# Attention scores in 64 by 64 products: queries and keys in place of the combined query-key weights

## The chip, the cores and the metric

The kernel runs on one core of one Trainium2 chip. The metric is device time in microseconds (us) for one execution. The time before is the median of three runs. One more execution was profiled, and all rows below come from it.

## What is computed

An audio tower: 64 sequences of 64 steps pass through a signature layer (running sums of outer products up to depth 4), then attention with 8 heads of 64 within each sequence, then a routed feed-forward layer with 8 experts and a shared one. The part that the change touches, cut from the reference:

```python
# h: (64, 63, 128) out of the signature layer; x is its layer norm
qkv = x @ Wq.T                      # Wq = w_qkv / spectral norm * sigma, (1536, 128)
q, k, v = split(qkv, 3)             # each (b, n, 8 heads * 64)
dots = einsum('bhid,bhjd->bhij', q, k) * exp(temperature)
dots = where(eye, NEG_MAX, dots)    # a step does not attend to itself
attn = softmax(dots, axis=-1)
out  = einsum('bhij,bhjd->bhid', attn, v)
h    = h + out @ Wo.T + b_out
```

Per head the score is x Wq' Wk x', which can be had either from queries and keys (64 wide) or from the product Wq' Wk (128 by 128), taken once.

## The kernel before

The 4096 padded steps are 32 tiles of 128 rows; a tile holds two sequences of 64. The kernel is written engine by engine, each with its own order of instructions, and semaphores between them. After a start-up, one loop runs over the tiles, and each `iteration(i, ...)` works on several tiles at once: attention of tile i, projection of the signature features of tile i+2, the level sums and features of tile i+3, and layer norm, router and output of tiles i-1 and i-2. A shared feed-forward stage, then 39 sorted expert slabs, follow. Work sits where the code puts it; no scheduler moves it.

PSUM is eight banks, B[0] to B[7]. The names that matter:

- `weight_products` (L1237) multiplies query and key weights of each head in the start-up, 64 rows of weights at a time into banks 6 and 7; ScalarE copies them to `qkw` (L663). The same helper does the products of value and output weights, which stay.
- In `iteration` of TensorE (L1368): eight products of `qkw` with the tile `xT` into banks 5 and 6 (L1375), which ScalarE scales into `xqk` (L608). The router's logits of tile i-2 go to bank 4 (L1381), and VectorE copies them out (`keep_logits`, L936).
- `three(...)` makes the values-times-output product in halves of 512 columns, three matmuls each: the first into bank 7, the second into bank 5 (L1385, L1387). ScalarE copies both to `xvo` (L613), and SP moves them by head to `xvp` by DMA.
- `project(i + 2, lo, hi)` (L1280) is the projection of the features, cut into ten chunks of two or three matmuls that stand between the attention's steps. `accumulate` (L1316) sums the channels, after GpSimd's tree of additions.
- The scores (L1396): a bf16 matmul writes the mask into bank 4, then for each of the two sequences one fp32 product adds the scores of all eight heads: the 64 columns of `xT` as the loaded operand, 512 columns of `xqk` as the moving one, into 64 rows of the bank.
- VectorE takes the row maximum and subtracts it (L999, L1001), ScalarE the exponential, VectorE the sum and the division. PE transposes the result (L1425) and multiplies it with `xvp` one iteration later (`values`, L1358).
- At tiles 25 to 27 VectorE also does steps of the routing (`choose`, `running`, `place`) at the end of its iteration, and at `RANK_AT` (tile 26) PE ranks the early tiles into bank 6. From tile 28 GpSimd also issues the scatters of the early tiles' rows.

All matmuls go through the helper `mm`, so they share the line L1217.

## Time and profile before

| | us |
|---|---|
| median of three runs | 694.17 |
| the three runs | 692.53, 694.17, 695.29 |
| the profiled execution | 691.94 |
| its span on the core | 690.1 |

In the page PE stands for TensorE's matmuls, PEld for its weight loads, which run beside them. A matmul's end in the records is modelled: its last record's duration holds a tail that the next one overlaps, so the pace of a run of matmuls is read from the starts. In a timeline several like instructions are merged, with "x16" for their number, from the first start to the last end. An fp32 matmul leaves two records of each kind. The bf16 matmul of the mask has a load record, but no matmul record. The clock of TensorE was granted in full in the loop.

### The profile page before, as it was taken

What the parts mean: (1) busy time and instruction counts of PE and PEld (TensorE: products, weight loads), DVE (VectorE), ACT (ScalarE), POOL (GpSimd) and SP (SyncE); (2) the same over time, 40 slices, a digit from 0 to 9 for tenths busy, and PEclk for the clock granted to TensorE, in tenths of its full rate; (3) what the DMA queues carried; (4) which work ended last, traced back from release to release, by engine and by line L of the source; (5) the groups of instructions that cost most, each with busy time, mean ns of one, the idle gap of its engine ahead of it and who ended that gap; (6) DMA issues with size and microseconds to landing.
All of it is one profiled execution on the core that took longest, in us unless ns stands there. A gap on an engine that the chain in (4) does not pass through costs nothing.

```text
span 690.1 us, 13988 instructions
## 1 busy us (share of the span) xinstructions
PE 647.0 (94%) x3964; PEld 519.6 (75%) x3997; DVE 420.6 (61%) x1110; ACT 295.9 (43%) x702; POOL 322.1 (47%) x336
## 2 busy tenths in 40 slices
PE   5999999999999999999999999999789989999993
PEld 4677887788878888788877887776578957777772
DVE  7876666666666666766656666766436235455451
ACT  4234455434544445444454344443646334434340
POOL 2455454544545445444545444448534014545453
PEclk9999999999999999999999999999999999999997
DMA  8611344333634334343343431112354113232230
GB/s 308 270 35 31 78 104 95 90 93 76 146 83 99 84 80 118 77 107 76 93 105 83 100 77 39 34 36 73 99 195 138 43 46 44 37 44 39 39 40 5
DMA packets 70133, 59.70 MB, mean 87 GB/s; under 512 B 6752, under 2 KB 58848, under 8 KB 69728
## 3 DMA queue, kind: packets, MB, share of 16 engines
q1 hardware_dynamic: 63472, 55.21, 30.2%
q0 software_dynamic: 6640, 4.22, 4.4%
q8 instruction: 12, 0.20, 0.1%
q14 instruction: 9, 0.07, 0.0%
HBM read 16.78 MB, written 26.30 MB: 62 GB/s over the span
## 4 chain that ended last, share of the span: by engine, by line
PE 83%; DVE 6%; issue 4%; POOL 4%; DMA 1%; ACT 0%; SPq 0%; ACTq 0%; DVEq 0%; POOLq 0%
PE bank L1217 74%; PE bank L1539 3%; PE bank L1273 2%; PE bank L1426 2%; POOL sorted_rows L485 1%; POOL z L470 1%; PE bank L1522 1%; PE bank L1332 1%; PE bank L1323 0%; PE bank L1278 0%; POOL z L472 0%; PE bank L1277 0%; POOL out L558 0%; DVE utl L777 0%; DVE z L883 0%
## 5 line engine op out<-in xcount | busy, mean ns | idle before, releaser
L1217 PE MATMUL bank<-whigh,uth 128*128 128x512 f32 x512 | 169.1, 411 | 1.2 <-DVE lowt L777 1.2
L1217 PEld LDWEIGHTS bank<-whigh,uth 128*128 128x128 f32 x512 | 92.4, 190 | 28.0 <-issue 7.4
L558 POOL DMA_INDIRECT out<-prob,ids x39 | 60.9, 1561 | 94.0 <-ACT prob L740 92.5
L1217 PE MATMUL bank<-whigh,utl 128*128 128x512 f32 x256 | 101.6, 397 | 0.0
L479 POOL TENSOR_TENSOR rstd<-rstd,powers 128x1 f32<-128x1 f32 x64 | 35.3, 552 | 119.8 <-DVE rstd L870 64.5
L470 POOL TENSOR_TENSOR z<-z 128x512 f32<-128x512 f32 x32 | 42.3, 1323 | 90.9 <-DVE z L883 90.9
L1217 PE MATMUL bank<-xT,qkw 128*128 128x128 f32 x512 | 63.9, 279 | 0.0
L1190 DVE COPY xvp<-bank 128x512 f32<-128x512 f32 x39 | 27.0, 692 | 59.3 <-PE bank L1539 59.3
L1217 PEld LDWEIGHTS bank<-xT,qkw 128*128 128x128 f32 x512 | 61.3, 196 | 0.1
L1217 PEld LDWEIGHTS bank<-whigh,utl 128*128 128x128 f32 x256 | 48.4, 189 | 11.9
L883 DVE TENSOR_TENSOR z<-bank,v 128x512 f32<-128x512 f32 x64 | 44.1, 690 | 20.8 <-PE bank L1217 16.8
L1217 PE MATMUL bank<-whigh,vow 128*128 x117 | 49.0, 526 | 0.0
L628 ACT ACTIVATE prob<-prob 128x512 f32<-128x512 f32 x32 | 20.2, 633 | 66.4 <-DVE prob L1001 63.5
L610 ACT ACTIVATE xqk<-bank,fac 128x512 f32<-128x512 f32 x64 | 43.9, 690 | 7.2 <-PE bank L1217 5.7
L638 ACT COPY pt<-bank 128x512 f32<-128x512 f32 x32 | 18.8, 587 | 64.6 <-PE bank L1426 62.5
L729 ACT ACTIVATE z<-bank 128x512 f32<-128x512 f32 x39 | 23.3, 597 | 49.0 <-PE bank L1217 27.7
L465 POOL TENSOR_TENSOR e3l<-e,e3h 128x512 fp32r<-128x512 f32 x31 | 40.8, 1316 | 7.4 <-DVE xn L904 6.5
L1217 PEld LDWEIGHTS bank<-xvp,pt 128*64 128x64 f32 x512 | 30.1, 137 | 18.3 <-issue 18.3
L1217 PE MATMUL bank<-vow,xTh 128*128 128x512 f32 x128 | 42.9, 416 | 0.0
L892 DVE TENSOR_TENSOR h<-bank,tokb 128x128 f32<-128x128 f32 x32 | 9.3, 290 | 54.4 <-PE bank L1217 54.4
L1217 PE MATMUL bank<-xqk,xT 128*64 128x512 f32 x128 | 34.5, 618 | 8.4 <-DVE logits L938 4.2
L617 ACT COPY xvo<-bank 128x512 f32<-128x512 f32 x64 | 37.6, 587 | 10.5 <-PE bank L1217 8.9
(227 smaller groups left out, 1439.2 us busy)
## 6 DMA issues: line engine op xcount, KB each, us to landing
sorted_rows<-blank SPq DMA_DIRECT2D x24, 709.5 KB, 5.7
xvp<-xvo SPq DMA_DIRECT2D x128, 128.0 KB
w<-w_t SPq DMA_DIRECT2D x1, 4096.0 KB, 12.3
xvo<-sorted_rows SPq DMA_DIRECT2D x39, 64.5 KB, 1.7
w<-w_high SPq DMA_DIRECT2D x4, 512.0 KB, 6.5
x_columns<-x2t SPq DMA_DIRECT2D x32, 64.0 KB
xg_in<-x_columns SPq DMA_DIRECT2D x8, 256.0 KB
levels<-w_t SPq DMA_DIRECT2D x1, 2048.0 KB, 7.5
```

The source lines that it names most:

```text
L465: G.tensor_tensor(e3l[:], e3[:], e3h[:].bitcast(F32), ALU.subtract).then_inc(e3_lo, 1)
L470: G.tensor_tensor(z4[:], z[:, 0:4, :], z[:, 4:8, :], ALU.add).then_inc(tree, 1)
L479: G.tensor_tensor(rstd[:, n, 1:2], rstd[:, n, 0:1], powers[:, 0:1], ALU.pow) \
L558: nc.gpsimd.indirect_dma_start(out=out[:, :], out_offset=bass.IndirectOffsetOnAxis(ap=ids[:, j:j + 1], axis=0), in_=y[:, j % 2, :], in_off ...
L610: A.activation(xqk[:, :, 4 * n:4 * n + 4, :], B[5 + n][:].rearrange("p (s h k) -> p s h k", s=2, h=4), ACT.Copy, scale=fac[:, 1:2]).then_i ...
L617: A.copy(xvo[:, n, :, :].rearrange("p c d -> p (c d)"), B[7 - 2 * n][:]) \
L628: A.activation(prob[:], prob[:], ACT.Exp).then_inc(exp_done, 1)
L729: nc.scalar.activation(act[:, k, :], B[1 + 2 * k][:], ACT.Silu).then_inc(silu_done, 1)
L883: V.tensor_tensor(z[:, cs, :], B[1 + half][:].rearrange("p (c d) -> p c d", c=4), spread(v[:, bass.ds(s, 1), cs].rearrange("p o c -> p (o ...
L1190: V.tensor_copy(hidT[:, k, :, :].rearrange("p c t -> p (c t)"), B[5][:]).then_inc(hT_sb, 1)
L1217: return T.matmul(out_, lhsT, rhs, start=start, stop=stop)
L1539: last = T.transpose(B[5][:, col(c)], hid[:, k, col(c)], ident)
```

## The change

The query-key products of the weights go. Instead the weights for queries and keys are loaded as they are, transposed, into `wqk` (one DMA of 512 KB in SP's queue, ahead of the shared expert's), and each iteration makes queries (bank 5) and keys (bank 6) with eight products of 128 by 128 by 128. ScalarE scales the queries and copies the keys into `qk`, in which a pair of heads takes the two halves of the partitions.

The scores become one fp32 product per head and sequence: 64 by 64 by 64, 16 of them. The head's half of the partitions picks the rows of the array, the sequence its columns, and the heads of a pair write two banks, 5 and 6. The mask is written in two halves into these. VectorE reads the scores from both banks in one instruction; for that the eight banks are one tensor.

Bank 4 is free of scores and takes the second half of the values-and-output product. It also holds the logits, so the wait for their copy (`lg_sb`) moves from the mask to this product, and `project(i + 2, 0, 1)` moves ahead of it. The early ranks go to bank 4.

TensorE, start of a loop iteration, before (`vow` is the values-and-output weight, `whigh` the projection's, `z,sq` the sum over channels, `gateT` the router's):

```order
L1217 MATMUL bank<-xT,qkw 128x2x64 x7
L1335 REGISTER_ALU
L1217 MATMUL bank<-gateT,x2t 128x8 [waits x2T_sb]
L1382 REGISTER_ALU
L1217 MATMUL bank<-vow,xTh 128x512 [waits h2_done,xT_lo]
L1217 MATMUL bank<-vow,xTh 128x512
L1217 MATMUL bank<-vow,xTl 128x512
L1386 REGISTER_ALU
L1217 MATMUL bank<-vow,xTh 128x512 [waits xqk_sb]
L1217 MATMUL bank<-vow,xTh 128x512
L1217 MATMUL bank<-vow,xTl 128x512
```

And after, the same place:

```order
L1218 MATMUL banks<-vow,xTl 128x512
L1281 ISA
L1282 REGISTER_ALU [waits z_sb]
L1283 ISA [waits u4_hi]
L1218 MATMUL banks<-whigh,uth 128x512 [waits u4_lo]
L1218 MATMUL banks<-whigh,uth 128x512
L1218 MATMUL banks<-whigh,utl 128x512
L1218 MATMUL banks<-vow,xTh 128x512 [waits logits_sb]
L1218 MATMUL banks<-vow,xTh 128x512
L1218 MATMUL banks<-vow,xTl 128x512
```

The second `vow` product stood straight behind the first; now the projection's chunk stands between them, and the wait for the logits in front of the second.

TensorE around the scores, before:

```order
L1217 MATMUL bank<-z,sq 128x128 [waits tree]
L1396 MATMUL bank<-mask,ident_b 128x512 [waits logits_sb,xqk_sb]
L1217 MATMUL bank<-xqk,xT 64x512 x2
L1360 ISA [waits xvo_sb]
L1217 MATMUL bank<-xvp,pt 64x128 [waits probT_sb,xvo_by_head]
L1217 MATMUL bank<-xvp,pt 64x128 x7
```

And after:

```order
L1218 MATMUL banks<-z,sq 128x128 [waits tree]
L1394 MATMUL banks<-mask,ident_b 128x256 [waits queries_keys_sb]
L1394 MATMUL banks<-mask,ident_b 128x256
L1218 MATMUL banks<-qk 64x64 x16
L1402 REGISTER_ALU
L1358 ISA [waits xvo_sb]
L1218 MATMUL banks<-xvp,pt 64x128 [waits probT_sb,xvo_by_head]
```

Two wide products have become sixteen narrow ones, and the mask no longer waits for the logits.

The core of the diff:

```diff
@@ SP, loads
+            sp.dma_start(wqk[:].rearrange("p a c m -> p (a c m)"), wqk_t).then_inc(ld_qk, 16)
             sp.dma_start(sw1_in, sw1_t).then_inc(ld_sw, 16)
...
-            sp.wait_ge(ww_psum, 4)
+            sp.wait_ge(ww_psum, 2)
@@ ScalarE, iteration
-                for n in range(2):
-                    a.wait_ge(g_psum, 2 * i + (n + 1))
-                    A.activation(xqk[:, :, 4 * n:4 * n + 4, :],
-                                 B[5 + n][:].rearrange("p (s h k) -> p s h k", s=2, h=4),
-                                 ACT.Copy, scale=fac[:, 1:2]).then_inc(g_sb, 1)
+                a.wait_ge(g_psum, 2 * i + 1)
+                A.activation(qk[:, 0, :, :].rearrange("p c t -> p (c t)"), B[5][:], ACT.Copy,
+                             scale=fac[:, 1:2]).then_inc(g_sb, 1)
+                a.wait_ge(g_psum, 2 * i + 2)
+                A.copy(qk[:, 1, :, :].rearrange("p c t -> p (c t)"), B[6][:]).then_inc(g_sb, 1)
...
-                    A.copy(xvo[:, n, :, :].rearrange("p c d -> p (c d)"), B[7 - 2 * n][:]) \
+                    A.copy(xvo[:, n, :, :].rearrange("p c d -> p (c d)"), B[7 - 3 * n][:]) \
@@ ScalarE, start-up
-            for n in range(2):
-                a.wait_ge(ww_psum, n + 1)
-                A.copy(qkw[:, 4 * n:4 * n + 4, :].rearrange("p h d -> p (h d)"), B[6 + n][:]).then_inc(qkw_sb, 1)
@@ VectorE, iteration
-                sc = B[4][:].rearrange("p (c k) -> p c k", k=LEN)
-                V.tensor_reduce(rowmax[:], sc, AX, ALU.max).then_inc(soft, 1)
+                sc = banks[:, 5:7, 0:PAIRS * LEN].rearrange("p n (c k) -> p n c k", k=LEN)
+                row_max = rowmax[:].rearrange("p (n c) -> p n c", n=2)
+                V.tensor_reduce(row_max, sc, AX, ALU.max).then_inc(soft, 1)
                 d.wait_ge(soft, i + 1)
-                V.tensor_tensor(prob[:], sc, spread(rowmax[:], 2, [P, HEADS, LEN]), ALU.subtract) \
+                V.tensor_tensor(prob[:].rearrange("p (c n) k -> p n c k", n=2), sc,
+                                spread(row_max, 3, [P, 2, PAIRS, LEN]), ALU.subtract) \
                     .then_inc(shifted, 1)
@@ TensorE, iteration
-                for hd in range(HEADS):
-                    by_head = B[5 + hd // 4][:].rearrange("p (s h k) -> p h s k", s=2, h=4)
-                    last = mm(by_head[:, hd % 4, :, :], qkw[:, place(hd), :], xT[:])
-                    if hd % 4 == 3:
-                        last.then_inc(g_psum, 1)
+                for n in range(2):
+                    for c in range(PAIRS):
+                        last = mm(B[5 + n][:, col(c)], wqk[:, n, c, :], xT[:])
+                    last.then_inc(g_psum, 1)
...
                 three(B[7][:], x, [vow[:, n, 0:512] for n in range(2)]).then_inc(vo_psum, 1)
-                pe.wait_ge(g_sb, 2 * i + 1)
-                three(B[5][:], x, [vow[:, n, 512:] for n in range(2)]).then_inc(vo_psum, 1)
                 if u:
                     project(i + 2, 0, 1)
+                if prev and older:
+                    pe.wait_ge(lg_sb, i - 1)
+                three(B[4][:], x, [vow[:, n, 512:] for n in range(2)]).then_inc(vo_psum, 1)
                 if acc:
                     accumulate(i + 1)
                 pe.wait_ge(g_sb, 2 * i + 2)
-                if prev and older:
-                    pe.wait_ge(lg_sb, i - 1)
-
-                T.matmul(B[4][:], ident_b[:], mask[:], start=True, stop=False)
-                for s in range(2):
-                    last = mm(B[4][col(s, LEN), :], xT[:, col(s, LEN)],
-                              xqk[:, s, :, :].rearrange("p h k -> p (h k)"), False, True)
+
+                for n in range(2):
+                    half_ = slice(n * PAIRS * LEN, (n + 1) * PAIRS * LEN)
+                    T.matmul(B[5 + n][:, 0:PAIRS * LEN], ident_b[:], mask[:, half_], start=True, stop=False)
+                for c in range(PAIRS):
+                    for n in range(2):
+                        head = col(n, HEAD_DIM)
+                        for s in range(2):
+                            last = mm(B[5 + n][col(s, LEN), col(c, LEN)], qk[head, 0, c, col(s, LEN)],
+                                      qk[head, 1, c, col(s, LEN)], False, c == PAIRS - 1)
                 last.then_inc(s_psum, 1)
...
-                    mm(B[6][:, 0:n], below, oh_early[:].rearrange("p t e -> p (t e)"))
-                    mm(B[6][:, n:2 * n], ones, oh_early[:].rearrange("p t e -> p (t e)")).then_inc(rank_psum, 1)
+                    pe.wait_ge(vo_sb, 2 * i + 2)
+                    mm(B[4][:, 0:n], below, oh_early[:].rearrange("p t e -> p (t e)"))
+                    mm(B[4][:, n:2 * n], ones, oh_early[:].rearrange("p t e -> p (t e)")).then_inc(rank_psum, 1)
@@ TensorE, start-up
-            weight_products(B[6:8], PAIRS, wqkv_sb[:, 0:PAIRS, :])
...
-            pe.wait_ge(qkw_sb, 2)
...
+            pe.wait_ge(ld_qk, 16)
```

## Rows read from the trace of the kernel before

**Rows 1.** The page, the chain that ended last, shares of the span by engine.

```profile
PE 83%; DVE 6%; issue 4%; POOL 4%; DMA 1%; ACT 0%; SPq 0%; ACTq 0%; DVEq 0%; POOLq 0%
```

**Rows 2.** The chain in 200:240: shares by line, then start, duration, what.

```profile
by line: PE bank L1217 91.2%; PE bank L1273 3.0%; PE bank L1426 2.2%; issue 1.1%; PE bank L1323 0.8%; PE bank L1278 0.8%; PE bank L1277 0.8%; PE bank L1332 0.6%
...
204.93 4.73 PE bank L1217 x31
...
219.17 4.73 PE bank L1217 x31
```

**Rows 3.** Timeline of one iteration: start, us, engine, line, what [idle before <- releaser].

```profile
214.53 1.95 PE L1217 MATMUL bank<-xT,qkw 128*128 128x128 f32 x16
...
217.24 0.63 PE L1217 MATMUL bank<-vow,xTh 128*128 128x512 f32 x2
...
217.95 0.63 PE L1217 MATMUL bank<-whigh,uth 128*128 128x512 f32 x2
...
219.17 0.20 PEld L1217 LDWEIGHTS bank<-xqk,xT 128*64 128x64 f32 x4 [0.32 <-issue]
219.17 1.08 PE L1217 MATMUL bank<-xqk,xT 128*64 128x512 f32 x4
...
220.08 1.04 PE L1217 MATMUL bank<-xvp,pt 128*64 128x128 f32 x16
...
221.05 0.30 PEld L1217 LDWEIGHTS bank<-whigh,uth 128*128 128x128 f32 x2 [0.17 <-issue]
...
221.75 0.63 ACT L628 ACTIVATE prob<-prob 128x512 f32<-128x512 f32 x1 [1.94 <-DVE prob L1001]
```

**Rows 4.** Scores' records in 10 ns windows: window, length, busy (x records in it).

```profile
219.19:219.20 0.01, 0.01 (x2) 0.01 (x2) 0.00 (x0) 0.00 (x0) 1.00 0.00 0
...
219.63:219.64 0.01, 0.01 (x2) 0.00 (x0) 0.00 (x0) 0.00 (x0) 1.00 0.00 0
219.67:219.68 0.01, 0.01 (x4) 0.00 (x0) 0.00 (x0) 0.00 (x0) 1.00 0.00 0
```

**Rows 5.** The values' records in such windows: PE, then PEld, DVE, ACT.

```profile
220.18:220.19 0.01, 0.01 (x2) 0.01 (x2) 0.00 (x0) 0.00 (x0) 1.00 0.00 0
220.20:220.21 0.01, 0.01 (x4) 0.01 (x4) 0.00 (x0) 0.00 (x0) 1.00 0.00 0
...
220.31:220.32 0.01, 0.01 (x6) 0.01 (x4) 0.00 (x0) 0.00 (x0) 1.00 0.00 0
```

**Rows 6.** Timeline of the start-up: PE's wait, ScalarE's copies, and products of 64 rows.

```profile
11.59 0.47 PE L1217 MATMUL bank<-e3h,before_r 128*128 128x512 f32 x1 [1.15 <-DVE e3l L847]
...
16.73 1.09 ACT L665 COPY qkw<-bank 128x512 f32<-128x512 f32 x2
...
20.81 1.16 PE L1217 MATMUL bank<-woutT,w 64*128 64x128 f32 x16
...
20.81 0.97 PEld L1217 LDWEIGHTS bank<-woutT,w 64*128 64x128 f32 x16 [0.36 <-issue]
```

**Rows 7.** Values of the last tile in 10 ns windows, right after a DMA wait.

```profile
501.36:501.37 0.01, 0.01 (x3) 0.01 (x4) 0.00 (x0) 0.00 (x0) 1.00 0.00 0
501.39:501.40 0.01, 0.01 (x4) 0.01 (x3) 0.00 (x0) 0.00 (x0) 1.00 0.58 205
```

**Rows 8.** Waits of PE in 400:510: total us, times, longest.

```profile
PE bank L1217 <- DVE logits L938: 4.2, 3, 1.5
```

**Rows 9.** Timeline: VectorE's low features and a logits copy, with PE's next load.

```profile
216.34 0.62 DVE L777 TENSOR_TENSOR lowt<-bank,lowt 64x128 fp32r<-64x128 f32 x2
...
450.89 0.17 DVE L938 COPY logits<-bank 128x8 f32<-128x8 f32 x1
...
451.17 0.10 PEld L1396 LDWEIGHTS bank<-mask,ident_b 128*128 128x128 bf16 x1 [1.32 <-issue]
```

**Rows 10.** The chain in 455:482: where it leaves PE and comes back.

```profile
460.54 0.70 DVE z L883
...
479.08 0.50 PE bank L1217 x2
```

More of the change, by code:

```diff
@@ L89, in build @@
 def build(nc, x_next, x_prev, w_low, w_high, tok_b, wqkv, u_qkv, wout_t, u_columns, b_out,
-          scalars, gate_t, w13_t, w2_t, sw1_t, sw2_t, square, mask_c, steps, out):
+          scalars, gate_t, wqk_t, w13_t, w2_t, sw1_t, sw2_t, square, mask_c, steps, out):
     with ExitStack() as ctx:
@@ L112, in build @@
         tokb = sb("tokb", [P, DIM])
-        qkw = sb("qkw", [P, HEADS, DIM])
+        wqk = sb("wqk", [P, 2, PAIRS, P])
         vow = sb("vow", [P, 2, HEADS * DIM], F32R)
@@ L182, in build @@
         xTl = sb("xTl", [P, P], F32R)
-        xqk = sb("xqk", [P, 2, HEADS, LEN])
+        qk = sb("qk", [P, 2, PAIRS, P])
         xvo = sb("xvo", [P, 2, PAIRS, DIM])
@@ L230, in build @@
                      prob[:].rearrange("p a b -> p (a b)"), z4[:].rearrange("p a b -> p (a b)"))
-        wide = (z[:].rearrange("p c d -> p (c d)"), xqk[:].rearrange("p a b c -> p (a b c)"),
+        wide = (z[:].rearrange("p c d -> p (c d)"), qk[:].rearrange("p a b c -> p (a b c)"),
                 xvp[:].rearrange("p a b c -> p (a b c)"), tail)
@@ L272, in build @@
         y = late(2, DIM)
-        B = [ctx.enter_context(nc.psum_tensor(f"bank{n}", [P, 512], F32)) for n in range(8)]
-        ld_x, ld_before, ld_sq, ld_c, ld_w, ld_wo, ld_sn, ld_w13, ld_w2, ld_sw = (
+        banks = ctx.enter_context(nc.psum_tensor("banks", [P, 8, 512], F32))
+        B = [banks[:, n, :] for n in range(8)]
+        ld_x, ld_before, ld_sq, ld_c, ld_w, ld_wo, ld_sn, ld_qk, ld_w13, ld_w2, ld_sw = (
             sem(f"loaded_{n}") for n in ("x", "before", "square", "const", "attention", "attention_out", "norms",
-                                       "w13", "w2", "shared"))
+                                       "query_key", "w13", "w2", "shared"))
         ld_sig = [sem(f"loaded_signature{c}") for c in range(UC + 1)]
@@ L284, in build @@
         w_hi, w_lo = sem("signature_weights_hi"), sem("signature_weights_lo")
-        ww_psum, ww_hi, ww_lo, qkw_sb = (sem("weight_products_psum"), sem("value_out_weights_hi"),
-                                         sem("value_out_weights_lo"), sem("query_key_weights"))
+        ww_psum, ww_hi, ww_lo = (sem("weight_products_psum"), sem("value_out_weights_hi"),
+                                 sem("value_out_weights_lo"))
         sw_hi, sw_lo = sem("shared_weights_hi"), sem("shared_weights_lo")
@@ L300, in build @@
         xT_hi, xT_lo = sem("xT_hi"), sem("xT_lo")
-        g_psum, g_sb, vo_psum, vo_sb = sem("xqk_psum"), sem("xqk_sb"), sem("xvo_psum"), sem("xvo_sb")
+        g_psum, g_sb, vo_psum, vo_sb = sem("queries_keys_psum"), sem("queries_keys_sb"), sem("xvo_psum"), sem("xvo_sb")
         s_psum, soft, shifted, exp_done = sem("scores_psum"), sem("row_max"), sem("shifted"), sem("exp_done")
@@ L630, in iteration @@
                     a.wait_ge(rank_psum, 1)
-                    A.copy(ranks_early.rearrange("p n m -> p (n m)"), B[6][:, 0:2 * EARLY * EXPERTS]) \
+                    A.copy(ranks_early.rearrange("p n m -> p (n m)"), B[4][:, 0:2 * EARLY * EXPERTS]) \
                         .then_inc(rank_kept, 1)
@@ L668, in _ @@
             for n in range(2):
-                a.wait_ge(ww_psum, n + 3)
+                a.wait_ge(ww_psum, n + 1)
                 A.copy(vow[:, 0, n * 512:(n + 1) * 512], B[5 - n][:]).then_inc(ww_hi, 1)
@@ L1220, in col @@
                 return slice(c * n, (c + 1) * n)
-            def place(hd):
-                return hd % 2 * PAIRS + hd // 2
             pe.wait_ge(ld_before, 16)
@@ L1589 @@
 _IN = ["x_next", "x_prev", "w_low", "w_high", "tok_b", "wqkv", "u_qkv", "wout_t", "u_columns",
-       "b_out", "scalars", "gate_t", "w13_t", "w2_t", "sw1_t", "sw2_t", "square", "mask_c", "steps"]
+       "b_out", "scalars", "gate_t", "wqk_t", "w13_t", "w2_t", "sw1_t", "sw2_t", "square", "mask_c", "steps"]
 def kernel(x, L0_tok_W, L0_tok_b, L0_attn_w_qkv, L0_attn_u_qkv, L0_attn_sigma_qkv, L0_attn_w_out,
@@ L1637 @@
         "gate_t": np.asarray(L0_ffn_gate_w).T,
+        "wqk_t": wqkv[:2 * INNER].T,
         "w13_t": np.concatenate([w1, w3], axis=1).transpose(2, 0, 1),
```

## The prediction

> **What bounds the kernel now.** First the page: TensorE (PE) holds 83% of the chain that ended last [rows 1]. An average hides stages, so next the chain inside the tile loop: PE's lines are nearly all of it, 91.2% the matmul helper's alone, and the same piece comes back after 14.24 us (204.93 to 219.17) [rows 2]. In the loop, then, time is what PE's queue takes, in order; work taken from VectorE or ScalarE gives nothing. The third view is PE's row of one iteration [rows 3], where the edited parts can be priced. Fourth come the places where PE is not the bound: three stalls of 4.2 us in all on the copy of the logits (L938) [rows 8], and a stretch from 460.54 to 479.08 in which the chain leaves PE for VectorE and GpSimd [rows 10].
>
> **What a pass is.** An fp32 matmul shows as two loads and two matmuls, two passes. The eight projections at 214.53 are 16 passes in 1.95 us less the 0.27 of the last one's tail, 0.112 us each for 128 columns [rows 3]. The change keeps eight products of 128x128x128 there, so this part costs what it did. The two output runs of 64 become one of 128; a pair of the values' passes, which write one run of 128, steps 0.11 too [rows 5], so I take nothing.
>
> **The scores before.** Four passes of 512 columns into 64 output rows. At 219.19 two are in progress, at 219.63 still two, at 219.67 four [rows 4]: both halves of the columns of the array stream together, and the second pair starts at about 219.65. The next product's load stands at 220.08, so a pair of passes streams 0.43 us, and the first took 0.05 more because its load was not hidden (219.17 to 219.65). From load to load: 219.17 to 220.08, **0.91 us**.
>
> **The scores after.** 16 products of 64x64x64, 32 passes of 64 columns, on four quarters of the array. The nearest rows are the values' products (two column halves, 128 columns a pass): two in progress at 220.18, four at 220.20, six at 220.31, so a pair starts every 0.11 us [rows 5], and the 16 passes take 1.04 less the last tail of 0.27 [rows 3]. The other split, by rows, stands in the start-up: 16 passes with 64 rows of weights each, into two banks, loads over 0.97 us, matmuls over 1.16 less 0.27, so 0.12 a pair at the most with the first load in it, and loads of 128 columns overlap each other there as well [rows 6]. So each kind of half runs at the pace of its own stream with the other half beside it. What no row shows is both splits at once. Bounds: if all four quarters stream together, a step is half of 0.11, as 64 is half of 128 columns, and 32 passes are 8 steps, 0.44 us. If no quarter overlaps another, a pass costs 0.055 (the same 0.11 over two), 1.76 us. I take the lower end: the rows show both splits free of each other, and the two starts of a pair lie within 0.02 us [rows 5].
>
> Around them the array changes its shape once more than before. After the values' last pair (start 220.08 + 7 x 0.11 = 220.85, end 0.11 later, 220.96) the next load waits until 221.05 [rows 3]: 0.09 for the change, and 0.05 for a load of 64 columns that nothing hides, as at 219.17. So from score load to values' stream: 0.05 + 0.44 + 0.09 + 0.05 = 0.63 against 0.91, 0.28 less. I give back 0.02 for the mask, which is now two matmuls of 256 in place of one of 512 with one more load, and 0.02 for four starts a step in place of two. **Gain 0.24 us an iteration.**
>
> The Trainium skill, "TensorEngine Tiling (Array Packing)", section Key Properties, says that a change of tiling mode drains the engine; the trace agrees, and the 0.09 above is its price here.
>
> **Where it counts.** Iterations 0 to 28 run at PE's pace; 29 begins at about 461, and it and 30 lie in the stretch that GpSimd's scatters set [rows 10]; 31 may count or not. 29 x 0.24 = **7.0 us**.
>
> **What the new order costs.** Before, the three stalled iterations did the second half of the values-and-output product (three passes, 217.24 to 217.95 in the ordinary iteration, 0.71) [rows 3] and the sum of the channels (0.22, two passes of 0.11) ahead of the wait for the logits, beside VectorE's routing steps. Now bank 4 holds that product, so the wait stands in front of it, and both come after the release: 0.93 us each, **3 x 0.93 = 2.8 us** lost. VectorE's release itself does not move: its chain starts from the transposes of the iteration before. In the ordinary iteration the logits' copy stands right behind the remainders that end at 216.96 [rows 9], and takes 0.17, and the wait, now due at 217.95, costs nothing; behind it in PE's queue stand the sum, the masks and the scores.
>
> The first chunk of the projection moves ahead of that product, from 217.95 to 217.24. It needs the last low part of the features, and VectorE ends that at 216.34 + 0.62 = 216.96. PE sees an end of VectorE 0.11 us later (450.89 + 0.17 = 451.06, then 451.17) [rows 9], so the load can start at 217.07 and, at 0.11, is in by 217.18: 0.06 us ahead. I take nothing, but this cover is thin.
>
> ScalarE's second copy to xvo comes some 0.7 us later, and behind it the low features, keep_x2 and the cast of e3. All of these had slack: the exponential that follows them waited 1.94 us for VectorE [rows 3]. SP's second pair of head moves is queued behind a wait for the attention of the tile before, which ends later than that copy. The key copy needs no scale and ScalarE is off the path: nothing. The banks 5 and 6 are now also the scores' banks: PE's next write to them waited for the transposed probabilities already, which come after VectorE's reads. VectorE reads as many elements as before.
>
> **Start-up.** Removed: 16 passes on PE, ahead of a wait of 1.15 us for VectorE at 11.59 [rows 6], so hidden; two ScalarE copies, 1.09 us from 16.73, beside PE and VectorE, which then do other work [rows 6]; and the wait for them. Added: one load of 512 KB in SP's queue, one issue ahead of the shared weights, long before its first use at 44. Bounds: 0 to 1.1 us gained. I take 0.
>
> **Sum.** -7.0 + 2.8 = -4.2 us. The profiled execution took 691.94 us (span 690.1 and 1.84 around it), 2.23 under the median of the three runs; the difference is of the same size for both, so from the median: 694.17 - 4.2 = **690.0 us**.
>
> **Rivals.**
> *Two at a time.* The queue gives a pass only so fast, or lets only two tiles run together. Where PE's queue was empty, after a DMA wait, the partner of a pair came 0.03 us behind: three in progress at 501.36, four at 501.39 [rows 7]. At 0.03 a pass 32 passes are 0.96 us; at half of 0.055, 0.88 us. Against it: where PE came from other work, partners start within 0.02 [rows 5], and in the ordinary iteration no wait ends in the 1 us ahead of the scores. With 0.88, 0.44 more than taken, -0.24 becomes +0.20, 29 x 0.20 = 5.8, plus 2.8: +8.6, 702.8 us; with 0.96, 705.1 us. **This one is slower than before.** It decides from 0.018 us a pass: 32 of them are 0.58, the group 0.81 with the terms above, 0.10 under 0.91, and 29 x 0.10 only pays the 2.8 back.
> The Trainium skill, "TensorE: Matmul & The Clock Gate", section "Wait — 56ns, not 53.3ns?", has a rule that speaks for it: successive matmuls start no closer than about 25 ns however few columns they have. Taken for every pass, that is 0.80 us for the scores, an estimate from that page, and some 700 us in all; its chance is within this rival's. The pairs of [rows 5] start closer than that, so between two halves the trace does not bear it out; for four quarters no row here shows it.
> *One at a time.* 32 x 0.055 = 1.76: 1.32 more than taken, +1.08 an iteration, 31.3 + 2.8, 728 us. For it: products with both splits are in no row. Against: each split alone overlaps fully.
> *A new wait takes the gain.* The 0.06 us ahead of the moved chunk turns negative by 0.05 to 0.15, in 27 iterations 1.4 to 4 us: 691.4 to 694.0, no change. For it: the chain transposes, ScalarE's two casts, VectorE's three remainders has no slack of its own.
> *It does not do what it says*: the loss in the stalled iterations is smaller, since something else is late there too, and the gain stays whole (0.28, 31 iterations, and 1.1 at the start): 694.17 - 8.7 - 1.1 + 1 = 685.4.
>
> **Chances.** Quarters together, 0.55; two at a time 0.22; one at a time 0.10; the new wait 0.13. The range holds the first, second and fourth with their ends: 686 to 705.5 us. A measurement of this kernel can tell about 0.5% from no change, 3.5 us: faster is below 690.7, slower above 697.6. The forecast stands close to that edge, so the first case gives 0.34 to faster and 0.20 to no change, the fourth 0.13 to no change; the rivals with wide passes give 0.32 to slower, and 0.01 is put there for the unforeseen: 0.34, 0.33, 0.33.
>
> **What would show it.** In the profile of the changed kernel: the score group from its first load to the values' load, 0.6 us if right, 1.0 if two at a time, 1.9 if one; in 10 ns windows, four passes of qk starting within some 0.03 us; a period of 14.0 us in place of 14.24; the three stalls on the copy of the logits summing to 7.0 us in place of 4.2, with the second product behind them; no idle time ahead of whigh at the moved chunk. Wrong it would be if the period rose, if PE shows a wait for VectorE's remainder in every iteration, or if the clock in the loop were granted below 1.00.

## The result, and the profile after

The changed kernel took **695.7 us** (median of 13 runs, 693.59 to 696.71), the kernel before, beside it, 693.06 us (13 runs, 691.65 to 695.29). The ratio is 1.0032, with a 95% interval of 1.0019 to 1.0044: slower by 0.3%, where 690.0 us had been forecast. The forecast started from the first three runs of the kernel before, 694.17 us; the median of the 13 is 1.1 lower. The profiled execution took 696.58 us, with a span of 694.8 us and a mean granted clock of 0.98; that of before had a span of 690.1.

The loop shows what was forecast. This is the chain inside it, the answer to [rows 2] (start, us, what):

```profile
203.67 4.42 PE banks L1218 x59
...
217.69 4.42 PE banks L1218 x59
...
```

The same piece comes back after 14.02 us; before it was 14.24. From iteration 2 to 26 the starts of the iterations lie 14.00 to 14.02 apart. The answer to the scores in [rows 3], from PE's row (start, us, line, what):

```profile
217.30 0.38 PE L1394 MATMUL banks<-mask,ident_b 128*128 128x256 bf16 x2
217.62 0.69 PE L1218 MATMUL banks<-qk 64*64 64x64 f32 x32
218.24 0.98 PE L1218 MATMUL banks<-xvp,pt 128*64 128x128 f32 x14
```

From the first score to the first value pass: 217.62 to 218.24, **0.62 us**, where 0.91 stood and 0.63 was worked out. In 10 ns windows (window, length, PE busy with the records in progress, clock) the score records pile up:

```profile
217.70:217.71 0.01, 0.01 (x4) 1.00 0.00 0
...
217.74:217.75 0.01, 0.01 (x8) 1.00 0.00 0
...
217.86:217.87 0.01, 0.01 (x16) 1.00 0.00 0
```

The first of the 32 records starts at 217.62, the eighth at 217.74, the last at 218.09. Between the eighth and the last lie six steps of four, 0.058 us each: one start every 15 ns on average. All 32 start within 0.48 us, and the values' first pass follows 0.15 later. No wait of PE stands between 60 and 400 us, so the moved chunk of the projection cost none either.

So the time must have gone elsewhere. It helps to cut both executions at the starts of the iterations (the first projection of queries and keys, in PE's row) and to compare pieces, in us. "again" is the changed kernel in another set of runs (a_again, below):

| piece | forecast change | before | after | change | again | change |
|---|---|---|---|---|---|---|
| start-up, to iteration 0 | 0 | 44.31 | 45.63 | +1.32 | 44.68 | +0.37 |
| iterations 0 to 25 | -6.24 | 369.67 | 363.43 | -6.24 | 363.56 | -6.11 |
| iterations 26 to 28 | +2.07 | 47.13 | 52.26 | +5.13 | 50.74 | +3.61 |
| iterations 29 and 30 | 0 | 27.51 | 30.54 | +3.03 | 27.56 | +0.05 |
| from iteration 31 to the end | 0 | 201.48 | 202.94 | +1.46 | 202.36 | +0.88 |
| span | -4.2 | 690.1 | 694.8 | +4.7 | 688.9 | -1.2 |

The first 26 iterations gave exactly what was forecast. Everything that is missing lies in the start-up and from iteration 26 on. The waits of PE between 410 and 465 us, answering [rows 8] (total us, times, longest):

```profile
PE banks L1218 <- DVE logits L937: 5.8, 3, 2.0
```

And this follows the first of these waits, in PE's row of iteration 26:

```profile
414.45 0.82 PE L1218 MATMUL banks<-vow,xTh 128*128 128x512 f32 x2 [1.83 <-DVE logits L937]
415.07 0.63 PE L1218 MATMUL banks<-vow,xTl 128*128 128x512 f32 x1
...
415.92 0.64 PE L1394 MATMUL banks<-mask,ident_b 128*128 128x256 bf16 x2
416.48 1.13 PE L1218 MATMUL banks<-qk 64*64 64x64 f32 x32
417.54 1.47 PE L1218 MATMUL banks<-xvp,pt 128*64 128x128 f32 x16
```

The scores take 1.06 us here and not 0.62, and the two masks 0.56 from start to scores and not 0.32: TensorE runs at about half speed. The windows around the first and the third stall say so (window, length, PE busy, granted clock, DMA):

```profile
412.00:416.00 4.00, 2.17 (x9) 0.87 0.00 0
416.00:420.00 4.00, 4.00 (x57) 0.70 0.02 4
...
448.00:452.00 4.00, 2.89 (x23) 0.64 0.00 0
450.00:454.00 4.00, 4.00 (x56) 0.69 0.00 0
```

The mean granted clock falls below 1.00 behind these two stalls (it has two levels, 1.2 and 2.4 GHz, that is 0.50 and 1.00). In the kernel before, with stalls of at most 1.5 us in the same three iterations, the windows around them read:

```profile
416.00:420.00 4.00, 2.71 (x14) 1.00 0.00 0
432.00:436.00 4.00, 2.58 (x14) 1.00 0.00 0
448.00:452.00 4.00, 2.53 (x14) 1.00 0.00 0
```

In the changed kernel the stall of iteration 27 lies between the other two in length (1.83 and 1.99 us), and the clock did not fall behind it:

```profile
432.84 0.74 PE L1218 MATMUL banks<-vow,xTh 128*128 128x512 f32 x2 [1.96 <-DVE logits L937]
```

```profile
432.00:436.00 4.00, 3.16 (x56) 1.00 0.00 0
```

The other new thing is in iterations 29 and 30, in the rows of three engines around the scores of tile 30:

```profile
480.81 0.69 PE L1218 MATMUL banks<-qk 64*64 64x64 f32 x32
...
481.56 0.96 POOL L487 DMA_INDIRECT sorted_rows<-x,pos  x1 [0.30 <-issue]
...
481.77 0.15 DVE L899 TENSOR_SCALAR rstd<-meanvar 128x1 f32<-128x1 f32 x1
...
482.82 0.96 POOL L487 DMA_INDIRECT sorted_rows<-x,pos  x1 [0.31 <-issue]
...
483.81 0.57 POOL L481 TENSOR_TENSOR rstd<-rstd,powers 128x1 f32<-128x1 f32 x1
...
484.51 0.69 DVE L999 TENSOR_REDUCE rowmax<-banks 128x8 f32<-128x512 f32 x1 [2.60 <-remote]
```

The values' record starts at 481.43, so the scores' stream is over by about 481.5. VectorE is free at 481.92. Yet the row maxima start at 484.51, and the wait is put down to "remote", a releaser that the profile cannot place. In the kernel before they started at once:

```profile
480.84 0.69 DVE L999 TENSOR_REDUCE rowmax<-bank 128x8 f32<-128x512 f32 x1
```

So three suspects: the stalls, the clock behind them, and signals that come late.

### The profile page after: what moved, and what is told of

The parts are those of the page before. It is cut to its first block, busy times and chain, and to the rows that moved or that the text cites. A ratio compares the mean times of both kernels' runs of the same rounds, so it can differ in the third digit from the quotient of the medians.

```text
span 694.8 us, 15813 instructions
## 1 busy us (share of the span) xinstructions
PE 649.1 (93%) x4908; PEld 532.8 (77%) x4909; DVE 420.6 (61%) x1110; ACT 291.8 (42%) x700; POOL 320.7 (46%) x336
## 4 chain that ended last, share of the span: by engine, by line
PE 85%; DVE 7%; issue 2%; POOL 2%; ACT 1%; another core or an unknown queue 1%; DMA 0%; SPq 0%; ACTq 0%; POOLq 0%; DVEq 0%
PE banks L1218 75%; PE banks L1540 3%; PE banks L1271 2%; PE banks L1428 2%; PE banks L1394 1%; PE banks L1523 1%; PE banks L1330 1%; POOL z L472 1%; PE banks L1276 0%; PE banks L1321 0%; PE banks L1275 0%; DVE utl L776 0%; DMA sq<-square 0%; DVE ident_b L1063 0%
## 5 line engine op out<-in xcount | busy, mean ns | idle before, releaser
L1218 PE MATMUL banks<-whigh,uth 128*128 128x512 f32 x512 | 169.0, 411 | 1.6 <-DVE lowt L776 1.6
L1218 PEld LDWEIGHTS banks<-whigh,uth 128*128 128x128 f32 x512 | 92.0, 190 | 28.1 <-issue 7.7
L1218 PE MATMUL banks<-whigh,utl 128*128 128x512 f32 x256 | 101.7, 397 | 0.0
L1218 PE MATMUL banks<-xT,wqk 128*128 128x128 f32 x512 | 64.1, 280 | 0.0
L1218 PEld LDWEIGHTS banks<-xT,wqk 128*128 128x128 f32 x512 | 61.3, 196 | 0.0
L1218 PEld LDWEIGHTS banks<-whigh,utl 128*128 128x128 f32 x256 | 48.5, 189 | 11.8
L882 DVE TENSOR_TENSOR z<-banks,v 128x512 f32<-128x512 f32 x64 | 44.1, 691 | 20.4 <-PE banks L1218 16.3
L1218 PE MATMUL banks<-vow,xTh 128*128 128x512 f32 x128 | 44.4, 428 | 5.8 <-DVE logits L937 5.8
L1218 PE MATMUL banks<-whigh,vow 128*128 x117 | 49.0, 526 | 0.0
L1218 PE MATMUL banks<-levels,xvp 128*128 x312 | 41.4, 276 | 0.7 <-ACT prob L739 0.5
```

The lines of the kernel that those rows point to most:

```text
L882: V.tensor_tensor(z[:, cs, :], B[1 + half][:].rearrange("p (c d) -> p c d", c=4), spread(v[:, bass.ds(s, 1), cs].rearrange("p o c -> p (o ...
L1218: return T.matmul(out_, lhsT, rhs, start=start, stop=stop)
```

## Experiments

All were made in six sets (the result above is set 1), with runs of the kernel before beside them. Each of sets 2 to 6 ran on one chip; which chip set 1 ran on is not on record. Sets 3 and 6 ran on the same one. The kernel before took 693.06, 693.12, 693.81, 693.06 and 693.42 us in the sets with several runs of it: it does not depend on the set. The changed one does, as the first experiment shows.

### The changed kernel, unchanged

Three further times, in sets 2, 3 and 4.

> The changed kernel once more, unchanged. Theory (the tail takes the gain): the profile shows again a period of 14.00 us in the middle, and iterations 26 to 30 together some 8 us longer than the kernel before, with TensorE's granted clock at 0.50 after the stalls on the logits copy of iterations 26 and 28, and the row maxima of tiles 29 and 30 starting 2 to 3 us after the scores end. Time about 695.7 us, ratio to before 1.002 to 1.005. Rival (one execution's accident): the falls of the clock or the late row maxima are in other places or absent, and the profiled execution is 2 us or more shorter than 696.6.

> The changed kernel unchanged, a third time. It took 695.7 us (profiled 696.58) at first and 691.1 (690.72) the second time, with the kernel before at 693.1 both times: in the first profile TensorE's clock fell behind the stalls of iterations 26 and 28 and the row maxima of tiles 29 and 30 came 2 and 2.7 us late, in the second it fell behind that of 28 alone and the row maxima were in time. Theory (two outcomes of one program, set when it is loaded): again one of the two, 690.5 to 692 or 695 to 696.5, each with its own signs. Rival (a spread of single executions): a median between, 692.5 to 694.

> The changed kernel unchanged, for the second control of the runs beside it. In its first and third execution signals of TensorE (scores of tiles 29 and 30, values, columns of x) reached VectorE, ScalarE and SyncE 2 to 2.7 us late in iterations 29 and 30, in the second in none; iterations 29 and 30 with it took 30.5 and 30.8 us against 27.6. If it depends on the loading, one of the two comes again: 695 to 697.5 with late signals, 690.5 to 692 without.

Set 2: 691.08 us, ratio 0.9979 (0.9966 to 0.9992). Set 3: 697.09, ratio 1.0038 (1.0021 to 1.0055). Set 4: 695.46, ratio 1.0032 (1.0020 to 1.0043). So the same program is 0.2% faster than before in one set and 0.3 to 0.4% slower in three. The loop is the same in all (period 14.00 to 14.04). The late part is not:

| iteration | before | set 1 | set 2 | set 3 | set 4 |
|---|---|---|---|---|---|
| 26 | 16.04 | 18.24 | 16.74 | 16.74 | 18.28 |
| 27 | 15.52 | 16.24 | 16.24 | 16.23 | 16.24 |
| 28 | 15.57 | 17.78 | 17.76 | 17.74 | 17.77 |
| 29 | 13.13 | 13.85 | 12.95 | 13.89 | 13.87 |
| 30 | 14.38 | 16.69 | 14.61 | 16.90 | 16.72 |

Iteration 26 has two lengths 1.5 us apart, with the same stall in each: in set 2 it is 1.83 us too, but the scores behind it take 0.63.

```profile
413.64 0.73 PE L1218 MATMUL banks<-vow,xTh 128*128 128x512 f32 x2 [1.83 <-DVE logits L937]
...
414.97 0.69 PE L1218 MATMUL banks<-qk 64*64 64x64 f32 x32
415.60 1.09 PE L1218 MATMUL banks<-xvp,pt 128*64 128x128 f32 x16
```

So the expectation of a_again held for the loop and for the fall behind iteration 28, and missed the rest: no fall behind 26, no late row maxima, 691.1 us in place of 695.7. Nor are there just two outcomes, as a_third supposed: set 3 has late signals and no fall behind 26. Late signals are in all nine profiles of sets 3, 4 and 6 taken of the changed kernel or its variants, as in that of set 1, and in none of the five of sets 2 and 5. Each variant is a program of its own, so the chip, or what else a set has in common, goes with them, and not the single execution. A spread of single executions as the whole cause is out too: the medians stand apart by 4 to 6 us, each from 7 runs or more.

### Taking the stall away

```diff
@@ ScalarE, iteration, behind the two copies of queries and keys
+                if prev and older:
+                    a.wait_ge(lg_psum, i - 1)
+                    A.copy(logits[:, bass.ds(i - 2, 1), :].rearrange("p o c -> p (o c)"), B[4][:, P:P + EXPERTS]) \
+                        .then_inc(lg_sb, 1)
@@ VectorE, iteration
-                if prev and older:
-                    keep_logits(i - 2)
```

> The changed kernel with the copy of the logits in ScalarE's row behind the two copies of queries and keys, and no longer on VectorE behind the routing steps. Theory (stalls on that copy): the waits of TensorE of 5.8, 3 and 2.0 us in iterations 26 to 28 and the stretches at 0.50 of the clock behind them go. Against a period of 14.00 these iterations were 4.2, 2.2 and 3.8 us long, 10.3 in all; VectorE is late for the row maxima of tile 26 by about 1 us all the same, so 7.5 to 9.5 us come off: 686 to 688 us, 4.5 to 7 us below the kernel before. Rival (the routing steps themselves are the price): the wait moves to the row maxima, and less than 3 us come off.

> The kernel before with the same copy of the logits moved to ScalarE. Its iterations 26 to 28 were 1.8, 1.3 and 1.3 us over its period of 14.245. Theory (stalls on that copy): 3.5 to 4.5 us come off, 688.5 to 690 us. Taken with the run of the changed kernel with this edit, the difference of the two is what the new scores alone are worth: 1 to 3 us for the changed kernel. Rival (the stalls are not worth more in the changed kernel): both kernels gain the same 4 us.

> The changed kernel with the logits copy on ScalarE, a second time, beside the plain changed kernel. Theory (stalls on that copy and the clock behind them): 8 to 10.5 us below the plain one whichever loading it meets, 682 to 688 us. Rival (the first run met a good loading): under 5 us below it.

> The kernel before with the logits copy on ScalarE, a second time, as the counterpart of the changed kernel with it, which took 682.6 us in one set (this one 689.05) and 686.6 in another. Theory (before is the same in every loading, only the changed kernel's tail is not): 688.5 to 689.5 us, ratio to before 0.9925 to 0.995.

| | set | this kernel | before beside it | ratio (95%) | beside it, without the edit |
|---|---|---|---|---|---|
| changed | 2 | 682.64 | 693.12 | 0.9844 (0.9826 to 0.9862) | 691.08 |
| changed | 4 | 686.62 | 693.06 | 0.9905 (0.9891 to 0.9919) | 695.46 |
| before | 2 | 689.05 | 693.12 | 0.9935 (0.9918 to 0.9953) | 693.12 |
| before | 5 | 688.75 | 693.42 | 0.9927 (0.9914 to 0.9940) | 693.42 |

The copy takes 0.17 us on ScalarE, right behind the key copy, and PE does not wait once from 400 to 450 us. First ScalarE's row of iteration 26, then the windows of PE in the same kernel (set 2):

```profile
410.42 0.59 ACT L614 COPY qk<-banks 128x512 f32<-128x512 f32 x1 [0.20 <-PE banks L1220]
410.90 0.17 ACT L617 COPY logits<-banks 128x8 f32<-128x8 f32 x1
```

```profile
400.00:414.00 14.00, 14.00 (x124) 1.00 0.18 43
414.00:430.00 16.00, 16.00 (x141) 1.00 0.16 38
430.00:446.00 16.00, 16.00 (x128) 1.00 0.23 54
```

The edit is worth 8.4 and 8.8 us to the changed kernel, 4.1 and 4.7 to the one before, as expected, though 682.64 us lies below the 686 to 688 that had been expected from the slower set 1. Iterations 26 to 28 now take 14.67, 14.05 and 14.25, against 14.90, 14.25 and 14.25 in the kernel before with the edit. The routing steps themselves do not bind, so that rival is out. Within set 2 the two kernels with the edit differ by 6.4 us, where 1 to 3 had been expected: the change's own worth where there are neither stalls nor late signals. The profiled spans differ by 6.0: start-up +0.5, iterations 0 to 25 -6.2, the rest -0.3.

**This version, the change with the logits copied by ScalarE, beats both kernels**: 1.6% under the kernel before in one set, 0.95% in another. Part of that is the edit's alone. Where signals come late (set 4, with 30.0 us for iterations 29 and 30 in place of 26.9) it is only about 2.1 us under the kernel before with the same edit, if that takes there what it took in set 5 (686.62 against 688.75).

### The clock behind the stall

The stall stays, but TensorE has work in it, of no use: products into the free half of a bank, ahead of the wait, in iterations 26 to 28 alone.

```diff
@@ TensorE, iteration, behind project(i + 2, 0, 1)
+                if late:
+                    for _ in range(16):
+                        mm(B[0][:, 0:P], wqk[:, 0, 0, :], xT[:])
```

> The changed kernel with 16 passes of 128 by 128 into a free part of PSUM ahead of the wait on the logits copy, in iterations 26 to 28 alone: 16 x 0.111 = 1.8 us, as long as the shortest of the three stalls (1.8 to 2.0 us), so that the stall stays and TensorE is busy in it. Theory (the clock is a price of its own): the granted clock stays at 1.00 from 26 to 28, and 1.4 us come off for each iteration in which it had fallen: 1.4 to 3 us below the plain kernel. Rival (the stall is all): no difference, or slower by what the passes overrun, under 0.5 us.

> The kernel before with the same 16 passes in iterations 26 to 28. Its stalls were 1.2 to 1.5 us and its clock did not fall there, so the passes overrun each stall by 0.3 to 0.6 us: 0 to 1.5 us slower. If it gains as the changed kernel does, the passes do something else than hold the clock.

This size was a mistake: an fp32 product is two passes, so 16 of them took 3.5 us (x32 in the trace, 411.99 to 415.47) and overran each stall. 699.45 us (ratio 1.0081) and 700.48 us (1.0089), both far over what was expected; they tell only that the kernel pays for the overrun. With 8 products, in set 4:

> The changed kernel with 8 products of 128 by 128 (16 passes by the trace, which shows 0.11 us for each pass, 1.8 us in all) ahead of the wait on the logits copy in iterations 26 to 28; the version with 16 products took 3.5 us for them and overran each stall by about 1.6 us. Theory (the clock is a price of its own): iteration 28 takes 16.1 to 16.4 us in place of 17.76, since the granted clock stays at 1.00, iterations 26 and 27 stay at 16.7 and 16.2, and the time is 1.2 to 1.8 us below the plain kernel's. Rival (the stall is all): 17.7 us again for iteration 28.

693.64 us, ratio 1.0008 (1.0000 to 1.0017), 1.8 us under the unchanged kernel beside it. Its iterations 26, 27 and 28 took 16.74, 16.25 and 16.25 us, beside 18.28, 16.24 and 17.77 without the filling, and the same windows as above now read:

```profile
412.00:416.00 4.00, 3.95 (x58) 1.00 0.00 0
416.00:420.00 4.00, 4.00 (x30) 1.00 0.37 85
...
448.00:452.00 4.00, 4.00 (x61) 1.00 0.14 32
450.00:454.00 4.00, 4.00 (x21) 1.00 0.58 133
```

Each fall costs **1.5 us** (18.28 - 16.74, 17.77 - 16.25). Filled with useless work, a stall of the same length is cheaper by that much. The rival, 17.7 us again for iteration 28, is out. The gain of 1.8 in the medians is less than 3.0. The other executions have no profile, but each has a mean granted clock: 0.980 to 0.982 in all twelve of the unchanged kernel, 0.985 or more in nine of the twelve with the filling and 0.981 in three. The start-up and the end move this mean too, so it does not count the falls.

When it falls was asked with a shift: 8 products ahead of iteration 0, so that every iteration starts later.

```diff
+            pe.wait_ge(xT_hi, 2)
+            for _ in range(8):
+                mm(B[5][:, col(0)], wqk[:, 0, 0, :], xT[:])
             iteration(0, True, True, True, False)
```

> The changed kernel with 8 more passes of 128 by 128 on TensorE ahead of iteration 0 (the first product of iteration 0 eight times over, 8 x 0.111 = 0.9 us), so that every iteration begins 0.9 us later. Theory (whether the clock falls behind a stall of 2 us depends on when the stall falls): other iterations among 26 to 28 show the fall than in the plain kernel sent with it, and the time moves by 0.9 us and some 1.5 us per fall more or less. Rival (it depends on the stall alone): the same iterations show it, and the time is 0.9 us over the plain kernel.

697.12 us in the median, as the unchanged kernel beside it (697.09), though iteration 1 begins 1.55 us later (16 passes again, not 8; 59.46 against 57.91). Iteration 28 took 16.26 us in place of 17.74, with a stall of the same length (2.0) and no fall in its windows; iteration 29 took 15.04 in place of 13.89.

```profile
446.00:450.00 4.00, 2.05 (x40) 1.00 0.00 0
448.00:452.00 4.00, 3.83 (x59) 1.00 0.00 0
```

So the stall alone does not decide. That the shift spared the clock is not shown: it is one profile, and its iteration 28 begins at 442.62 us, between those of profiles without the shift that have the fall (441.10 to 443.80). Seven profiles have the changed kernel's own order on TensorE, the four unchanged and three with moved scatters (below). The clock fell behind the stall of iteration 28 in all seven, behind that of 26 in four, and behind that of 27, which is as long, in none. In the three profiles of the next experiment's kernel, with the same three stalls, it fell behind 28 in one alone. What decides is open.

### Two quarters at a time

```diff
-                for c in range(PAIRS):
-                    for n in range(2):
+                for n in range(2):
+                    for c in range(PAIRS):
```

Neighbours in the queue now lie on the two quarters of one half of the rows.

> The changed kernel with the loop over the head of a pair outside the loop over the pairs, so that the 16 score products of one half of the rows are issued before the 16 of the other half; same products, same banks. Theory (four quarters at once need neighbours in the queue on four quarters): the group from the first score to the first value product takes 1.1 to 1.25 us in place of 0.62, the period 14.4 to 14.6, and the time rises by 10 to 16 us less what slack gives back, to 703 to 711 us. Rival (the order in the queue does not matter to the array): 0.6 to 0.7 us and no difference in time.

697.7 us in set 2, ratio 1.0066 (1.0048 to 1.0083), 6.6 us over the unchanged kernel in that set; period 14.29. The scores in PE's row:

```profile
220.26 0.98 PE L1218 MATMUL banks<-qk 64*64 64x64 f32 x32
221.17 1.09 PE L1218 MATMUL banks<-xvp,pt 128*64 128x128 f32 x16
```

0.91 us from the first score to the first value pass, not 0.62 and not 1.1 to 1.25 either; the period (14.4 to 14.6 expected) and the time (703 to 711) were put too high with it. Strictly two at a time would be 16 pairs, 0.9 us at 0.06 a pair from the first start to the last. In the 10 ns windows the 32 starts lie between 220.26 and 221.02, 0.76 us, against 0.48 with the pairs outside, so for a part of the group more than two quarters were at work. The 0.91 is just that of the kernel before: without the right order of the products the new scores gain nothing. The rival, that the order does not matter to the array, is out.

### Late signals

> The changed kernel with 21 of the 24 early scatters of GpSimd (tiles 3 to 23) taken out of iterations 29 to 31 and put behind iteration 31. The scatters end later and what needs the sorted rows may wait, so the total (697 to 715 us) says nothing; iterations 29 and 30 are read. Theory (signals of TensorE come late while GpSimd issues scatters): the row maxima of tiles 29 and 30 start within 0.2 us of the scores' end, iterations 29 and 30 take under 28 us together. Rival (the late signals have nothing to do with the scatters): 2 us late again wherever the plain kernel beside it shows it.

> The changed kernel with the scatters of GpSimd's iterations 28 and 29 (tiles 0 to 10) taken out and put behind iteration 31; those of iterations 30 and 31 stay. The total says nothing, since the last scatters come later. Theory (signals of TensorE come late while GpSimd issues scatters): the row maxima of tile 29 start within 0.2 us of the scores' end, iteration 29 takes 12.9 to 13.1 us in place of 13.9, and in iteration 30, where scatters are issued, the row maxima come 2.6 us late again. Rival (the scatters have no part in it): both late.

> The same kernel as a_scatter_30, in the hope of a loading with late signals; its first execution had none in either iteration. Theory (signals come late while GpSimd issues scatters): the row maxima of tile 29 in time (iteration 29 of 12.9 to 13.1 us), those of tile 30 2.6 us late. Rival: both late. Without any late signal it says nothing.

The edits only move GpSimd's scatters, for instance:

```diff
-                if is_tile(i, SCATTER_AT + 1):
-                    scatter(range(3, 6))
...
             root(1, ln2, TILES - 1)
+            scatter(range(3, EARLY))
```

a_scatter_late (714.89 us, its total says nothing) kept three scatters at the end of iteration 28, which run beside the scores of tile 29: row maxima late by 1.84. In iteration 30, with none, they were in time, and it took 11.33 us in place of 16.72. a_scatter_30 met a chip without late signals (set 5, 689.57 us) and told nothing. a_scatter_30b, the same kernel (705.67 us), met one that has them. There the scatters run from 479.28 to 483.02 and from 484.19 on; tiles 29 and 30 were in time and only tile 31 late. The scores in PE's row:

```profile
464.40 0.69 PE L1211 MATMUL banks<-qk 64*64 64x64 f32 x32
...
477.35 0.69 PE L1211 MATMUL banks<-qk 64*64 64x64 f32 x32
...
489.38 0.69 PE L1211 MATMUL banks<-qk 64*64 64x64 f32 x32
```

VectorE's row maxima of the same three tiles:

```profile
465.43 0.68 DVE L992 TENSOR_REDUCE rowmax<-banks 128x8 f32<-128x512 f32 x1
...
478.38 0.68 DVE L992 TENSOR_REDUCE rowmax<-banks 128x8 f32<-128x512 f32 x1
...
492.99 0.69 DVE L992 TENSOR_REDUCE rowmax<-banks 128x8 f32<-128x512 f32 x1 [1.77 <-remote]
```

And GpSimd's row beside the scores of tile 31:

```profile
489.38 0.96 POOL L487 DMA_INDIRECT sorted_rows<-x,pos  x1 [0.31 <-issue]
490.64 1.41 POOL L487 DMA_INDIRECT sorted_rows<-x,pos  x1 [0.30 <-issue]
```

The expectation had tile 30 late; its scores were over at 478.0, before the first scatter. The rule holds all the same, on these two executions: the lateness goes where the scatters go. In the sets that show it, signals of TensorE come late while GpSimd issues scatters. That this is enough is not so: the kernel before issues the same scatters beside the same scores.

> The kernel before once more, for its profile on this chip: if late signals are a matter of the chip alone, its row maxima of tiles 29 and 30 come 2 us late here too and iterations 29 and 30 take over 30 us (27.5 in its first profile); if they come with the changed kernel's code alone, it shows none.

694.06 us, ratio 1.0008 (0.9995 to 1.0021); iterations 29 and 30 took 27.66 us, no late signal. But this was set 5, whose chip showed none in any kernel, so it does not tell chip from code. Two other profiles do in part: the first one of the kernel before and b_filled, in set 3. Both have waits on "remote" later on (VectorE's additions at L1133, 4.1 and 4.0 us), as the changed kernel has in sets 1, 3 and 4 (2.5, 4.1 and 2.5) and not in set 2, and still their row maxima of tiles 29 and 30 were in time, with 27.5 us for both iterations in the first.

> The changed kernel with the score products of one half of the rows issued before those of the other, a second time; its first execution had no late signals (iterations 29 and 30: 27.5 us), but nor had the changed kernel beside it. Theory (late signals come from the loading, with whichever order of the scores): with late signals in the run beside it, rowmax of tiles 29 and 30 2 to 2.7 us late here too. Rival (four quarters at once are what makes them late): none here.

> The changed kernel with the scores of one half of the rows first, beside a run that shows whether this loading has late signals. Theory (whichever order of the scores): row maxima of tiles 29 and 30 2 to 2.7 us late where the run beside it has them. Rival (four quarters at once make them late): in time.

The first met set 5 again and told nothing (699.07 us). The second (703.98 us), beside a_scatter_30b, had them all: row maxima late by 1.93, 2.62 and 0.86 us. So it is not the four quarters at once. What in the changed kernel's code makes it liable, where the kernel before is not, stays **open**; no run kept the old scores with the new banks, or the other way round.

## Why the prediction was wrong

**The time of the scores: right.** 0.63 us had been worked out, 0.62 was measured, with 8 steps of four quarters; an iteration gained 0.24, and iterations 0 to 25 gave 6.24 us of 6.24. A step of four took 0.058 us where 0.055 had been taken, which the 0.02 given back for it covers. The rivals with two and one at a time were wrong as forecasts. That the order of the loops matters was in none of them: with the halves one after the other the group takes 0.91 us, between the 0.63 of four at a time and the 1.07 (0.63 + 0.44) of two.

The rule that was weighed there, from the Trainium skill, "TensorE: Matmul & The Clock Gate", section "Wait — 56ns, not 53.3ns?" (no two starts closer than about 25 ns), does not hold across quarters here: one started every 15 ns on average.

**A new wait at the moved chunk: did not come.** PE shows no wait there in any iteration between 60 and 400 us.

**Start-up: right within what a profile can tell.** It was put at 0 and shows +1.3. But five profiles of the kernel before and its variants start iteration 0 at 44.31 to 46.24 us, and those of the changed one without a shift at 44.58 to 45.89: the ranges overlap. In the first profile PE's first product starts at 4.43 us, before at 3.93.

**What the new order costs: the stall was right, its consequence was missing.** +0.93 per stalled iteration less the 0.24 gives +0.69; measured without a fall of the clock: +0.70, +0.71 and +0.68 (16.74, 16.23 and 16.25 against 16.04, 15.52 and 15.57). The three stalls were to sum to 7.0 us, from the 4.2 of PE's matmuls; PE's matmuls show 5.8 (its weight loads 7.1). The step that failed is this term, "3 x 0.93 = 2.8 us", which was priced as waiting time alone: for iterations 26 to 28 it makes +2.07 with the gain taken off, and +5.13 was measured in set 1, +3.61 in set 2. Behind a stall of 1.8 to 2.0 us, where 1.3 to 1.5 stood, TensorE's clock was in some iterations down at 1.2 GHz for the work that follows, 1.5 us each time; with the stall away, or filled, it was not. In set 1 that happened twice, 3.1 us. The prediction named "the clock in the loop granted below 1.00" among the things that would prove it wrong, and gave it neither a price nor a chance.

**Where it counts: wrong for iterations 29 and 30.** They were left out because GpSimd's scatters set that stretch. That they would get longer, by 3.0 us, was in no row of the kernel before: this is the late signals, in three of the four sets with the unchanged kernel. No rival had it.

**From iteration 31: +0.9 to +2.3 us** where 0 was put (+1.5, +0.9, +2.3 and +1.5 in sets 1 to 4). The fall of the clock after iteration 30, which before has too (0.58 at 488 to 490 and 0.57 at 490 to 492), is longer: 0.50 from 492 to 496, 0.78 from 496 to 498 in set 1. No experiment was made on it.

Put together for set 1: -6.24 + 2.07 as forecast, and +3.1 (clock), +3.0 (late signals), +1.3 (start-up), +1.5 (the end): +4.7 in the profiled executions. The medians differ by 2.6, since the profiled one of before was 1.1 under its median and that of the changed kernel 0.9 over. On the chip of set 2, without late signals and with the fall behind iteration 28 alone, the changed kernel took 691.08 us, near the forecast 690.0, but by luck: the change is -2.0 us there and not -4.2, and the 694.17 from which the forecast started was 1.1 too high.

## What to carry to other kernels

Price a stall of TensorE with what the clock does behind it, not as idle time only: here 0.5 us more of stall brought, in some iterations, 1.5 us more of slow work. When a change speeds up the loop that TensorE sets, look for the few iterations in which it waits for another engine's queue; move the small copy that releases it to an engine that is free at that moment, before judging the change, for it was worth 4 us to the old kernel and over 8 to the new. With products on quarters of the array, write them so that four neighbours lie on four quarters, and repeat the measurement on another chip before a difference of 0.3% is believed.

## What the runs showed of the hardware

- Products of 64 by 64 on four quarters, in two banks and fp32, stream together: four passes of 64 columns start every 0.058 us, all 32 within 0.48 us; with neighbours on two quarters only, within 0.76.
- The clock of TensorE fell to 0.50 behind some stalls of 1.8 to 2.0 us and not behind others of the same length in the same code: in seven profiles it fell seven times behind the third stall, four times behind the first and never behind the second. Behind stalls of 1.2 to 1.5 us it did not fall in the same three iterations of either profile of the kernel before.
- Signals of TensorE to VectorE came up to 2.7 us late in the changed kernel in sets 1, 3, 4 and 6 while GpSimd issued indirect DMAs (ScalarE too waited 2.4 to 2.6 us for "remote" in iteration 30 of sets 1, 3 and 4), and never in sets 2 and 5; sets 3 and 6 ran on one and the same chip. The kernel before, with the same DMAs, did not show it in set 3.
